# Attention, MLP and bidirectional Mamba on one core: work moved between the stages, the first MLP product in float32r, and the queries loaded in eight pieces

## The reference, cut to what matters

```python
# part 1
q, k, v1, v2 = (x @ W for W in (Wq, Wk, Wv1, Wv2))          # 8 heads of 32
att = softmax(einsum("bilhd,bljhd->biljh", q, k) / sqrt(32), axis=2)
out = einsum("biljh,bilhd,bljhd->bijhd", att, v1, v2)
h = layer_norm(x + out @ Wo)
x1 = layer_norm(relu(h @ W1 + b1) @ W2 + b2 + h)             # W1: 256 x 512
# part 2, for mh (along rows) and mv (along columns)
z, xBC, dt = split(x1 @ in_w.T)                              # 512, 640, 8
xBC = silu(causal_conv_4_taps(xBC))                          # x 512, B 64, C 64
dt = softplus(dt + dt_bias); dA = exp(-dt * exp(A_log))
h = h * dA + (dt * x) B ; y = h C                            # scan over 64 steps
y = (y + x * D) * silu(z)
y = y * rsqrt(mean(y * y) + 1e-5) * norm_w @ out_w.T
out = concat(y_v, y_h) @ fc_w.T + fc_b
```

## Time and profile before

| what | value |
|---|---|
| median of three runs | 2454.9 us |
| profiled execution, its own time | 2450.41 us |
| its span (first to last instruction) | 2448.2 us |
| PE, DVE busy over the span | 86%, 83% |
| ACT, POOL busy over the span | 53%, 50% |
| mean granted TensorE clock | 0.97 |

### The profile page before, as it was taken

The page is one execution under the profiler, slowest core; times in us unless marked ns, Lnnn a source line. Parts: engine busy times, 40 slices in busy tenths (PEclk is TensorE's granted clock), DMA queues, the critical chain, the costliest instruction groups (busy, mean ns, idle before and its releaser), DMA issues. The chain is left out here.

```text
span 2448.2 us, 43726 instructions
## 1 busy us (share of the span) xinstructions
...
## 2 busy tenths in 40 slices
...
DMA packets 299437, 204.51 MB, mean 84 GB/s; under 512 B 201697, under 2 KB 279009, under 8 KB 294625
## 3 DMA queue, kind: packets, MB, share of 16 engines
...
## 5 line engine op out<-in xcount | busy, mean ns | idle before, releaser
L285 DVE TENSOR_TENSOR att_av<-att_att,att_v2ps 128x2816 f32<-128x2816 f32 (+2 forms) x288 | 775.8, 2751 | 35.5 <-PE att_bank L464 32.7
L285 POOL TENSOR_TENSOR att_av<-att_att,att_v2sb 128x1280 f32<-128x1280 f32 x256 | 744.9, 2936 | 51.3 <-PE att_bank L464 46.7
L464 PE MATMUL att_bank<-att_av,att_w 128*32 128x512 f32 x4096 | 548.8, 617 | 221.7 <-DVE att_av L285 190.0
L464 PEld LDWEIGHTS att_bank<-att_av,att_w 128*32 128x32 f32 x4096 | 136.8, 111 | 572.7 <-issue 271.5
L630 ACT ACTIVATE att_ev<-att_bank 128x512 f32<-128x512 f32 x512 | 297.5, 595 | 270.2 <-PE att_bank L464 228.8
L1716 DVE SCALAR_TENSOR_TENSOR mb_cv<-mb_bank,mb_cw,mb_cv 128x504 f32<-128x504 f32 (+2 forms) x480 | 349.5, 733 | 74.1 <-ACT mb_cv L1534 63.4
L1403 PE MATMUL mb_bank<-mb_xT_hi,dt_win_hi 128*128 128x512 f32 x576 | 241.6, 420 | 37.3 <-DVE mb_ms L1760 24.2
L1332 POOL CAST mb_y_hi<-mb_y 128x1024 fp32r<-128x1024 f32 x64 | 67.4, 1053 | 369.3 <-DVE mb_y L1756 369.3
L1337 POOL TENSOR_TENSOR mb_y_lo<-mb_y,mb_y_hi 128x1024 fp32r<-128x1024 f32 x64 | 154.3, 2433 | 181.9 <-DVE mb_S L1725 181.9
L1403 PE MATMUL mb_bank<-mb_xT_lo,dt_win_hi 128*128 128x512 f32 x576 | 232.1, 403 | 0.0
L1403 PE MATMUL mb_bank<-mb_xT_hi,dt_win_lo 128*128 128x512 f32 x576 | 231.7, 402 | 0.0
...
## 6 DMA issues: line engine op xcount, KB each, us to landing
att_xin<-in_x SPq DMA_DIRECT2D x32, 512.0 KB, 4.6
...
mixed_t<-att_ev SPq DMA_DIRECT2D x1024, 8.0 KB
mb_dAb<-dA_rows SPq DMA_DIRECT2D x32, 512.0 KB, 6.4
mb_dAb<-dA_cols SPq DMA_DIRECT2D x32, 512.0 KB, 5.7
...
```

The source lines that it names most:

```text
L285: return eng.tensor_tensor(av[t % 2][:, :, d0:d1, :], a.unsqueeze(2).broadcast_to((P, 2, d1 - d0, N)), v2.unsqueeze(1).broadcast_to((P, 2, ...
L464: mm = pe.matmul(bank[r % NB][s * M:(s + 1) * M, :], w[i // WB % 2][:, i % WB, s, :], av[r // 2 % 2][:, i % 2, s * STRIP_D:(s + 1) * STRIP ...
```

## The change

Five edits.

1. `load_first` issues the queries in eight DMAs of 256 KB (64 partitions x 1024 columns). In attention's steps it is no longer called: the eight pieces are issued in steps 18, 21, 24, 27, 35, 38, 41 and 44, and the first keys in steps 47 and 50.
2. W1 is split into float32r parts by POOL, h's transposed chunk by ACT (`hT_hi`) and DVE (`hT_lo`, between the two halves of W2's sum). Each group `h @ W1` is six float32r products in place of two in float32.
3. The weights `out_w`, `fc_w` and `norm_w` are loaded behind chunk 7 of the MLP; POOL sums fc's halves, PE folds between the last two x1 chunks, ACT scales into `wf_hi`, DVE makes `wf_lo`. The results stay in memory that both blocks share.
4. POOL splits x1's first chunk out of the MLP's own transposed copy (`x1T`), so the Mamba stage neither loads, turns nor splits chunk 0, and PE begins with chunk 0's first group.
5. The first two scans of Mamba's first chunk stand between its taps; the DMAs at the stage's start are in another order (the decay's store before the small weights).

```diff
@@ attention: ACT
-            def load_q(n):
+            def load_q(n, piece):
                 need(act, scored, n * NG)
-                for b in range(B):
-                    act.dma_start(q[b * 64:(b + 1) * 64, :],
-                                 qk_dram[n * 64:(n + 1) * 64, b * N * N:(b + 1) * N * N]).then_inc(q_loaded, 16)
+                b, cols = piece % B, N * N // 4
+                lo = piece // B * cols
+                act.dma_start(q[b * 64:(b + 1) * 64, lo:lo + cols],
+                              qk_dram[n * 64:(n + 1) * 64, b * N * N + lo:b * N * N + lo + cols]).then_inc(q_loaded, 16)
             def load_first(n):
-                load_q(n)
+                for piece in range(8):
+                    load_q(n, piece)
...
-                if n + 1 < PAIRS and m == 20:
-                    load_first(n + 1)
+                if n + 1 < PAIRS and m in Q_AT:      # (18, 21, 24, 27, 35, 38, 41, 44)
+                    load_q(n + 1, Q_AT.index(m))
+                if n + 1 < PAIRS and m in K_AT:      # (47, 50)
+                    load_k(n + 1, K_AT.index(m))
@@ MLP: SP
+                if c == 7:
+                    for d in range(2):
+                        for dst, src in (out_w[d], fcw[d], normw[d] and their sources):
+                            sp.dma_start(dst, src).then_inc(fold_w_loaded, 16)
@@ MLP: POOL
+            pool.wait_ge(w_loaded, 32)
+            for k in range(KT):
+                pool.tensor_copy(w1_["hi"][:, k], w1[:, k]).then_inc(w1_split, 1)
+            pool.wait_ge(w1_split, KT)
+            for k in range(KT):
+                pool.tensor_tensor(w1_["lo"][:, k], w1[:, k], w1_["hi"][:, k], ALU.subtract).then_inc(w1_split, 1)
...
+            split_first_x1()     # waits x1T_copied >= KT; xT_hi = cast(x1T), xT_lo = x1T - xT_hi; x0_split
+            split_win(0)
+            split_win(1)
+            pool.wait_ge(fold_w_loaded, 16 * 6)
+            for d in range(2):
+                pool.tensor_tensor(fcw[d][:, 0:KT, :], fcw[d][:, 0:KT, :], fcw[d][:, KT:, :], ALU.add).then_inc(fc_summed, 1)
@@ MLP: PE
             def times_wo(c, u):
-                need(pe, hT_ready, 2 * c)
+                need(pe, hT_lo_ready, 2 * c)
             def mlp(c, u):
-                pe.wait_ge(hT_ready, 2 * c + 2)
+                pe.wait_ge(hT_lo_ready, 2 * c + 2)
...
-                    for k in range(KT):
-                        mm = pe.matmul(HID_[m][:, :], w1[:, k, m * P:(m + 1) * P], hT[u][:, k, :],
+                    for n, (k, xn, wn) in enumerate([(k, xn, wn) for k in range(KT) for xn, wn in SPLIT]):
+                        mm = pe.matmul(HID_[m][:, :], w1_[wn][:, k, m * P:(m + 1) * P], hT[xn][u][:, k, :],
...
+            pe.wait_ge(w1_split, 2 * KT)     # before chunk 0
             for c in (NCHUNK - 2, NCHUNK - 1):
                 turn_x1(c)
                 rows_of_dt(c)
                 turn_rows(c)
+                if c == NCHUNK - 2:
+                    fold(0)                  # the same 8 products each, into banks WO_ and HID_[2:4]
+                    fold(1)
@@ MLP: ACT
+                if c == 1:
+                    act.wait_ge(x0_split, 1)         # in copy_x1T
...
+                if c == NCHUNK - 2:                  # behind copy_x1T, copy_rows, copy_raw of chunk 14
+                    act.wait_ge(fold_w_loaded, 16 * 6)
+                    for d in range(2):
+                        act.wait_ge(folded, d + 1)
+                        for m in range(CT):
+                            act.activation(carried.wf[d]["hi"][:, m, :], FOLD_[d][m // 2][...],
+                                           ACT.Copy, scale=normw[d][:, m:m + 1]).then_inc(wf_hi_ready, 1)
@@ MLP: DVE
+            def low_of_hT(c, u):
+                if c < NCHUNK:
+                    for k in range(KT):
+                        dve.wait_ge(hT_hi_ready, 2 * c + k + 1)
+                        dve.tensor_tensor(hT["lo"][u][:, k, :], WO_[k][:, :], hT["hi"][u][:, k, :], ALU.subtract)\
+                            .then_inc(hT_lo_ready, 1)
...
+                    if half == 0:                    # in back(c), behind the first half's sum
+                        low_of_hT(c + 1, 1 - u)
@@ Mamba: SP
-            load_x1(0)
+            load_x1(1)
             (convolution weights)
+            sp.wait_ge(first_ready, 1)
+            store_decay(0, 0, HN)
             for d, w in enumerate(W2):
-                (out_w, fcw, dskip, normw; for d == 0 also x1's chunk 1, bias, store_decay, load_decay)
+                sp.dma_start(dskip[d][:, :], w["D"]).then_inc(skip_loaded, 16)
+            sp.dma_start(bias[:, :], W2[0]["fc_b"].partition_broadcast(P)).then_inc(skip_loaded, 16)
+            sp.wait_ge(dA_stored, 16)
+            load_decay(0)
             load_x1(2)
             load_decay(1)
@@ Mamba: PE
-            turn_first_decay()
-            turn_x1(0)
-            for i in range(NG):
+            group(0, 0)
+            pe.wait_ge(const_set, NCONST)
+            turn_first_decay()
+            for i in range(1, NG):
                 group(0, i)
-            fold(0)
@@ Mamba: DVE, first chunk (k == -1)
-            split_x1(0); sum_fc(0) ... scale_by_norm(0); sum_fc(1) ... scale_by_norm(1)
-                taps((3, 1), (3, 2), (3, 3), (4, 1), (4, 2), (4, 3))
+                if k == -1:
+                    scan(c, 0)
+                taps((3, 1), (3, 2), (3, 3))
+                if k == -1:
+                    scan(c, 1)
+                taps((4, 1), (4, 2), (4, 3))
```

More of the change, by code:

```diff
@@ L924, in mlp, with fold @@
                         turn_h(c + 1, 1 - u)
+            def fold(d):
+                pe.wait_ge(fc_summed, d + 1)
+                pe.wait_ge(*(hT_lo_ready, 2 * NCHUNK) if d == 0 else (hid_ready, FT * NCHUNK))
+                for m in range(CT):
+                    for k in range(KT):
+                        mm = pe.matmul(FOLD_[d][m // 2][:, (m % 2) * E:(m % 2 + 1) * E],
+                                       out_w[d][:, k, m * P:(m + 1) * P], fcw[d][:, k, :],
+                                       start=(k == 0), stop=(k == KT - 1))
+                mm.then_inc(folded, 1)
             times_wo(0, 0)
```

122 lines of the change are left out of this document (52 added, 70 removed).

## The result

The changed kernel takes 2421.8 us (median of 4 runs, 2419.9 to 2423.7), the kernel before 2454.3 on the same chip: a ratio of 0.9866, 95% interval [0.9849, 0.9883]. The prediction was 2427, range 2413 to 2441. The two profiled executions have spans of 2448.2 and 2421.9 us: 26.3 less, where 27.5 was forecast. The total came out right, but the parts did not, and this is what the rest is about. Where a run here fell into a slower state with a lower granted clock (one run of `w1_f32`, 2555.7 us, and one of `pool_late`, 2972.5), it is left out of the ratio.

The account below looks back on a forecast made before the run. Prediction: DVE bounds attention's steps, PE sets the MLP's pace, Mamba's first chunk is a chain. Terms -21 (MLP), +6.5 (folds), -9 (Mamba's start), -9 (steps), +5 (projections) sum to -27.5: 2454.9 becomes 2427 us, range 2413 to 2441.

Parts of the forecast that it names:

- W1 in float32r: MLP: PE's round falls by 1.47 us, less 0.15 for hops, over 16 chunks: 21 us gained, bounds 12 and 23.5.
- that the MLP's round stays above 19.3: MLP: a round staying above 19.3 us would show the prediction wrong; 18.4 to 18.7 was expected.
- no PE gap over 0.4: MLP: in a round of 18.4 to 18.7 us, PE was to show no gaps over 0.4 us.
- rival A: MLP: DVE's round is longer than PE's, hops shrink W1's gain to 8 us from 21; 2440 us, chance 0.14.
- POOL's split of W1: MLP's start: two casts and two subtractions on otherwise idle POOL cost nothing; if slow, a few us once.
- Folds, +6.5: End of the MLP: folds take 8.7 us, 1.7 us are covered; 6.5 us lost in sum, bounds 4.5 and 13.
- Mamba's start, -9: Mamba's first chunk: earlier taps and scans bring the second chunk's taps forward, 9 us gained, bounds 6 and 12.
- Steps, -9 of 10.7: Attention's steps: queries in pieces remove DVE's waits of 4.24 and 5.73 us; 9 us gained, bounds 4 and 10.7.
- Projections, +5: Beside v chunks 0 and 6: six more ACT issues each time make PE wait; 5 us lost, bounds 0 and 7.
- After the second chunk's taps, 0: Rest of the Mamba stage: DVE is hardly idle, so what is won before is kept to the end, nothing added.
- Rival D: MLP: PE gaps of about 3 us a chunk halve its clock, 58 us lost, not 21 gained; 2506 us, chance 0.05.

Follow-up runs that it names:

- w1_f32: The changed kernel with W1 and h's transposed chunk back in float32 and no low parts: 2429.5 us, ratio 0.9895 to the kernel before.
- pool_late: The changed kernel with POOL's split of W1 moved behind the first chunk's h, some 6 us later: 2423.6 us, ratio 0.9869 to the kernel before.
- scans_back: The changed kernel with the first two scans of Mamba's first chunk behind all its taps again: 2426.1 us, ratio 0.9882 to the kernel before.
- q_burst: The changed kernel with queries and keys loaded as before, two DMAs a time for queries, all at step 20: 2435.9 us, ratio 0.9927 to the kernel before.

## Why the prediction was right in total, and where it was not

- **W1 in float32r, "16 x 1.47 - 16 x 0.15 = 21 us gained"**: the term that failed. Its sum for a clean round was nearly right: 18.70 for 18.54, with PE's own saving 1.16 and not 1.47. But I compared DVE's and PE's rounds as two separate sums and missed the loop through ACT's queue, where the root stands ahead of the relus that W2 needs. Its 18.70 could be read before, in the second round, where PE has less to do. Once PE's round is as short, nothing is hidden any more, and POOL's splits and the dt steps, which 1.16 us of slack had covered, were paid in full; the late load, which is new, came on top. I had priced them at nothing. Measured: 4.4 in the trace from the second transposes on, with the load's 4.6 taken off, 3.8 lost ahead of them, and some 7 by the run. By the prediction's own sign, that the MLP's round stays above 19.3, this term was wrong in the mean (19.53) and right in the clean rounds; its sign of no PE gap over 0.4 failed too (1.15 and 2.84). This is close to rival A's 8 us, though by another cause than its hops.
- **POOL's split of W1, "I cost that at nothing"**: 3.8 us lost at the start between these two traces, since DVE stood still beside it (4.04 for 1.38); pool_late shows 2 to 3 of it. The same stretch differs by 1.5 to 2 us between profiles of one code.
- **Folds, +6.5**: +5.8 (5.5 to 7.0 over the traces with the same code), the rows as forecast (8.59 for 8.7). What I did not cost was their weights' DMA in the MLP, up to 3.5 us.
- **Mamba's start, -9**: -10.7, by the forecast's steps (5.3, 1.2 and 32.9 us into the stage), but by scans_back none of it by the scans.
- **Steps, -9 of 10.7**: -14.7 in the traces, and -15 by q_burst with the projections' loss in it, beyond my bound. I counted the waits right behind the bursts (4.24 + 5.73 and 0.7 around); the total of DVE's waits fell by 14.4, so 4 came from small waits elsewhere in the same steps. The bound was no bound: it summed the rows that I had picked.
- **Projections, +5**: +2.9 in the trace, known to some 2 us. PE's waits did grow to 7.01 and 7.63, 7.2 in sum; part of it is paid anyway, as said.
- **After the second chunk's taps, 0**: -8.9, unforeseen: 2.8 in the second chunk, some 4 from the place in SBUF (28.30 to 28.13), the rest not assigned. Part may be chance: the whole Mamba stage differs by 5 us between profiles of one code, and this one is among the shortest.

So the misses of +17 in the MLP and +4 at its start were made good by -6 in the steps, -2 each at the projections and Mamba's start, -1 at the folds and -9 behind the second chunk's taps. Rival D did not occur: no gap of 3 us stands in each chunk. The close sum was luck in part: of what made the MLP's 21 us good, 9 stand in no term of the forecast.
